# Placing pass of a graph kernel: two groups ahead on TensorE and ScalarE, one ahead on VectorE

## The reference

```python
for l in range(thetas.shape[0]):            # 3 layers
    xi, xj = x[src], x[dst]
    e = jax.nn.relu((xj - xi) @ thetas[l].T + xi @ phis[l].T)
    agg = jax.ops.segment_max(e, src, num_segments=N)
    agg = jnp.where(agg < -1e+30, 0.0, agg)
    mu, var = agg.mean(axis=0), agg.var(axis=0)
    x = jax.nn.relu((agg - mu) * jax.lax.rsqrt(var + BN_EPS) * gammas[l] + betas[l])
...
summ = jax.ops.segment_sum(msg, dst, num_segments=n)      # the later blocks sum over targets
```

## Time and profile before

| | us |
|---|---|
| median of three runs | 7011.9 (6974.34 to 7047.15) |
| the profiled execution, time | 7004.77 |
| its span, first to last instruction | 7003.0 |
| gathers of the second max-relative pass, first to last issue | 1298.8 to 1977.4 |

### The profile page before, as it was taken

One profiled execution on the slowest core, in us unless ns is written; L12 is line 12 of the kernel. 1 busy time (PEld: TensorE's weight loads), 2 busy tenths in 40 slices (PEclk: granted clock), 3 DMA queues, 4 the chain that ended last, 5 costly groups with the idle time before them and its releaser, 6 DMA issues. The chain is left out here.

```text
span 7003.0 us, 50568 instructions
## 1 busy us (share of the span) xinstructions
PE 2900.5 (41%) x12855; PEld 1680.4 (24%) x12907; DVE 3675.3 (52%) x8221; ACT 1725.5 (25%) x4386; POOL 3244.6 (46%) x3188
## 2 busy tenths in 40 slices
PE   4352001533354555699000597000300045677658
PEld 3211000311132222344000243000200024555435
DVE  8995444465555656444554433333543354565553
ACT  2270000122224555211232221323300022232222
POOL 0004776456536665100777301767277644555540
PEclk9696555755577777799555798555655567888879
DMA  0004554344434444233556433545255436878730
GB/s 8 1 1 148 184 187 161 101 153 168 157 109 140 160 161 151 94 153 139 178 195 208 167 134 136 197 168 193 92 181 193 167 131 203 270 260 276 248 98 19
DMA packets 379867, 1066.01 MB, mean 152 GB/s; under 512 B 74258, under 2 KB 162612, under 8 KB 333012
## 3 DMA queue, kind: packets, MB, share of 16 engines
q1 hardware_dynamic: 213586, 595.68, 22.6%
q0 software_dynamic: 164688, 466.32, 22.5%
q10 hardware_dynamic: 1330, 0.99, 0.0%
HBM read 541.40 MB, written 521.29 MB: 152 GB/s over the span
## 5 line engine op out<-in xcount | busy, mean ns | idle before, releaser
L790 POOL DMA_INDIRECT out_of<-table,index x936 | 966.5, 1033 | 706.6 <-DVE index L813 415.0
L790 POOL DMA_INDIRECT rows<-table,index x728 | 739.7, 1016 | 404.3 <-issue 217.4
L790 POOL DMA_INDIRECT rows<-typed_table,index x520 | 517.8, 996 | 587.2 <-DVE index L813 387.5
L3082 POOL DMA_INDIRECT qv<-qv_table,index x416 | 429.6, 1033 | 392.6 <-DVE index L3259 264.3
L790 POOL DMA_INDIRECT y<-typed_table,index x312 | 325.2, 1042 | 571.0 <-DVE index L813 462.7
L1460 PE MATMUL bank<-x,marks 128*128 128x416 f16 x1664 | 392.4, 400 | 315.2 <-ACT marks L1473 237.1
L825 DVE SCALAR_TENSOR_TENSOR y<-y,by_source_anew,out_of 128x256 f32<-128x256 f32 x897 | 436.4, 486 | 101.1 <-DMA out_of<-table,index 61.3
L1473 ACT ACTIVATE marks<-hot_block,x 128x128 f16<-128x128 f16 x1248 | 369.9, 386 | 346.0 <-DVE marks L1520 335.5
L2126 PE MATMUL bank<-weights,turned_y 128*128 128x512 f32 x800 | 357.5, 596 | 6.2 <-ACT turned_y L2186 5.5
L1933 PE MATMUL bank<-weights,out_of 128*128 128x512 f32 x800 | 349.7, 595 | 12.9 <-DVE weights L1978 12.9
L807 ACT ACTIVATE rows<-rows,by_target_weight 128x256 f32<-128x256 f32 x520 | 214.9, 494 | 518.8 <-DMA rows<-typed_table,index 270.0
(11 more groups left out here) (586 smaller groups left out, 7152.0 us busy)
## 6 DMA issues: line engine op xcount, KB each, us to landing
states<-y SPq DMA_DIRECT2D x156, 1024.0 KB
typed_table<-staged SPq DMA_DIRECT2D x400, 256.0 KB, 2.0
states<-state SPq DMA_DIRECT2D x78, 1024.0 KB
states<-out_of SPq DMA_DIRECT2D x78, 1024.0 KB
wide_states<-y SPq DMA_DIRECT2D x52, 1088.0 KB
near<-k_rows SPq DMA_DIRECT2D x416, 128.0 KB
out_of<-table,index POOLq DMA_INDIRECT x936
rows<-table,index POOLq DMA_INDIRECT x728
```

The costliest lines, as they stand in the source:

```text
L790: pool.indirect_dma_start(out=rows[h][:, u * D:(u + 1) * D], out_offset=None, in_=table, in_offset=bass.IndirectOffsetOnAxis(ap=index[h][: ...
L3082: pool.indirect_dma_start(out=qv[b][:, u * PAIR:(u + 1) * PAIR], out_offset=None, in_=qv_table, in_offset=bass.IndirectOffsetOnAxis(ap=ind ...
```

## The change

Each engine's order in PlaceTargets is shifted by whole groups.

- PE, in iteration g: codes and tally of group g+2, rank of g+1, compare of g+2, look_up of g.
- ACT, in iteration g: high half of g, then `hot_b` and `hot_r` of g+2.
- DVE, in the step of g: choose(g-1), mask(g+2), `part`(g), `run`(g), `same`(g+1), low(g).
- `hot_a` and `hot_r` get a third buffer.

The number of instructions and their shapes stay. Before the first group DVE now masks two groups and compares one.

The diff, cut to its core (the order of each engine):

```diff
             self.settle.tensor(pe)
-            over_groups(body)
+            for g in range(-2, GROUPS):
+                if g + 2 < GROUPS:
+                    meet(g + 2, g % 2)
+                    tally(g + 2, g % 2)
+                if 0 <= g + 1 < GROUPS:
+                    rank(g + 1, (g + 1) % 2)
+                if g + 2 < GROUPS:
+                    compare(g + 2, g % 2)
+                if g >= 0:
+                    pe.wait_ge(self.hot_row, 2 * g + 2)
+                    look_up(g, g % 2)
...
+            for g in range(-2, GROUPS):
+                if g >= 0:
+                    high(g, g % 2)
+                if g + 2 < GROUPS:
+                    mark(g + 2, g % 2)
...
     def mask(self, dve, g, h):
         nc, env, sort = self.sort.nc, self.sort.env, self.sort
-        if later(g):
+        if g >= 2:
             dve.wait_ge(self.crossed, 2 * g - 2)
+            dve.wait_ge(self.alike, 2 * g - 2)
...
-        self.mask(dve, 0, 0)
+        for g in range(2):
+            self.mask(dve, g, g)
+        self.match(dve, 0, 0)
         for g in range(RING + self.lead):
             self.group(dve, g, g % 2)
...
         if g > 0:
             self.choose(dve, g - 1, 1 - h)
-        if g < GROUPS - 1:
-            self.mask(dve, g + 1, 1 - h)
+        if g + 2 < GROUPS:
+            self.mask(dve, g + 2, h)
         dve.wait_ge(self.tallied, g + 1)
...
-        for s in range(2):
-            dve.wait_ge(self.alike, 2 * g + s + 1)
...
+        if g + 1 < GROUPS:
+            self.match(dve, g + 1, 1 - h)
         dve.wait_ge(self.cut_high, g + 1)
```

More of the change, by code:

```diff
@@ L1269, in ring @@
             return [buffer(stack, nc, name, cols, dt) for _ in range(count)]
-        self.mine, self.same, self.hot_b, self.hot_r = ring("mine", GROUP * P), ring("same", GROUP * P), ring("hot_b", GROUP * P), ring("hot_r", GROUP * P)
-        self.hot_a, self.run = ring("hot_a", GROUP * TILES), ring("run", TILES, FP32)
+        self.mine, self.same, self.hot_b, self.hot_r = ring("mine", GROUP * P), ring("same", GROUP * P), ring("hot_b", GROUP * P), ring("hot_r", GROUP * P, count=3)
+        self.hot_a, self.run = ring("hot_a", GROUP * TILES, count=3), ring("run", TILES, FP32)
         self.part, self.high_low, self.found = ring("part", GROUP * TILES, FP32), ring("high_low", 2 * GROUP * TILES), ring("found", 2 * GROUP * TILES, FP32)
@@ L1285, in _, with meet @@
         def _(pe):
-            def compare(g, h):
+            def meet(g, h):
                 now = sort.z[:, g * P:(g + 1) * P]
-                pe.wait_ge(self.masked, g + 1)
-                for s in range(2):
[L1290 to L1293, removed]
                 for s in range(2):
@@ L1353, in body @@
                     act.wait_ge(self.crossed, 2 * g + s + 1)
-                    if s == 0 and later(g):
-                        act.wait_ge(self.looked_up, g - 1)
-                    nc.scalar.activation(self.hot_r[h][:, s * half:(s + 1) * half], self.code_bank[s][:, 0:half], ACT.Relu,
+                    if s == 0 and g >= 3:
+                        act.wait_ge(self.looked_up, g - 2)
+                    nc.scalar.activation(self.hot_r[g % 3][:, s * half:(s + 1) * half], self.code_bank[s][:, 0:half], ACT.Relu,
@@ L1372, in mask, with match @@
-        hot_tiles(nc, env, self.hot_a[h][:], sort.col_a, g).then_inc(self.hot_tile, 1)
+        if g >= 3:
+            dve.wait_ge(self.picked, g - 2)
+        hot_tiles(nc, env, self.hot_a[g % 3][:], sort.col_a, g).then_inc(self.hot_tile, 1)
+    def match(self, dve, g, h):
+        nc, env = self.sort.nc, self.sort.env
+        half = GROUP * P // 2
+        for s in range(2):
+            dve.wait_ge(self.alike, 2 * g + s + 1)
+            if s == 0 and g >= 2:
+                dve.wait_ge(self.ranked, g - 1)
+            nc.vector.scalar_tensor_tensor(
+                out=bulk(self.same[h][:, s * half:(s + 1) * half], GROUP // 2), in0=bulk(self.alike_bank[s][:, 0:half], GROUP // 2),
+                scalar=float(NODE_BITS), in1=env.before[:].unsqueeze(1).broadcast_to([P, GROUP // 2, P]),
+                op0=ALU.is_equal, op1=ALU.mult).then_inc(self.compared, 1)
@@ L1407, in group @@
                                 op=ALU.add).then_inc(self.running, 1)
-        for s in range(2):
-            dve.wait_ge(self.alike, 2 * g + s + 1)
-            if s == 0 and later(g):
-                dve.wait_ge(self.ranked, g - 1)
-            nc.vector.scalar_tensor_tensor(
-                out=bulk(self.same[h][:, s * half:(s + 1) * half], GROUP // 2), in0=bulk(self.alike_bank[s][:, 0:half], GROUP // 2),
-                scalar=float(NODE_BITS), in1=env.before[:].unsqueeze(1).broadcast_to([P, GROUP // 2, P]),
-                op0=ALU.is_equal, op1=ALU.mult).then_inc(self.compared, 1)
+        if g + 1 < GROUPS:
+            self.match(dve, g + 1, 1 - h)
         dve.wait_ge(self.cut_high, g + 1)
```

34 lines of the change are left out of this document (16 added, 18 removed).

## The result

The changed kernel takes 7054.2 us (median of 20 runs, 7025.0 to 7091.4) against 7011.1 us for the kernel before on the same chip: 1.0068 times as long, 95% interval 1.0048 to 1.0087. That is 43 us slower, above the whole predicted range, which ended at 7025. The profiled execution has a span of 7070.2 us.

What follows compares the result with a forecast made beforehand. DVE with its waits for PE was taken to set the second max-relative pass's pace. From 7005 us, 56 gained in the loop and 6 lost before it gave 6955, or 6962 from the median; forecast 6960, range 6900 to 7025.

Steps and rivals of the forecast that it cites:

- part 3: Look-up in the second pass's loop: its 5.2 us chain fits 6.0 us; the wait before `found` is 70 to 100 us.
- Part 1: Tally asked for two groups ahead: DVE's 144.5 us of waits before `part` are gained, all but nothing left.
- Part 2: Comparison one group ahead and masks two ahead: `same` had no idle time before it, so nothing gained or lost.
- Part 4: Gathers come next in the loop: 530 to 550 us, middle 540, a gain of 56; ends 492 and 596.
- Part 5: Five groups before the loop, without a fold as cover: loss of 6 us, between a gain of 10 and a loss of 15.
- (a): Rival: the wait moves from `part` to `found`, DVE's 226 us of waits stay, loop 596 us, total 7015; chance 0.24.
- (b): Rival: gathers bound the loop at the pace of a pass without companion, 492 us, total 6910; chance 0.22.
- (c): Rival: look-up late in every group because of ACT's order, held codes, tally and look-up adding up; 7090 us, chance 0.08.

Runs made afterwards that it cites:

- e5: Changed kernel with seven of eight gathers of the second max-relative pass left out from its fifth group on; 6685.5 us, one run.
- v1: Changed kernel with TensorE's look-up of g right behind rank of g+1, ahead of compare, crossed and tally of g+2; 1.0059 of the kernel before.
- v4: Changed kernel with `hot_b` of g+2 ahead of the high half of g on ScalarE, `hot_r` still behind it; 1.0069 of the kernel before.
- e8: Changed kernel with POOL allowed three groups of gathers ahead of the folds in the second pass instead of four; 1.0063 of the kernel before.
- e10: Changed kernel with POOL stopped after every second group (16 gathers) of the second pass until the gathers have landed; 6832.8 us, 0.9873 of the kernel before.
- e18: The changed kernel as it is, run again on another chip; 6285.7 us, 1.0007 of the kernel before.
- e16: Changed kernel with POOL stopped after every fourth group (32 gathers) of the second pass; 1.0048 of the kernel before.
- v3: Changed kernel with look-up ahead of compare, crossed and tally, choose(g-1) ending VectorE's group, four buffers of `hot_a` and `hot_r`; 1.0023 of the kernel before.

## Why the prediction was wrong

**The step that failed is part 3, the look-up**, which took "70 to 100 us" for the wait before `found`, and bounded it by "all of the 144.5 us could come back here". It measured 261.3, above even the 70.0 + 144.5 = 214.5 of that bound. That the chain fits into its cover of 6.0 us was right, and e5 shows it: without most of the gathers `found` waits 0.6 us in all. (The 5.2 us of the chain are rather 5.4: rank, compare and look-up of the earlier trace rows are 0.37 + 1.03 + 0.51 = 1.9 us, not 1.7.) What was wrong was the nature of a hold. I took it from the earlier trace rows as a delay of 5 to 6 us that adds to one operation and can be hidden by asking two groups ahead. It is more like a closed door: reports of TensorE pile up, and most of the long ones come only when POOL has run out of gathers. In the table of reports above tally, rank, compare, look-up and codes were issued within 2.0 us; the first was learned of 16.1 us after its issue and the other six within 0.23 us of each other, 1.5 us later. Asking earlier does not help against that, as v1 to v4 show.

Why the sum of the waits grew, from 214.5 to 261.3 us, is argued and not shown. DVE can run ahead only over reports that are already in, and while it does, it writes indices and so gives POOL more gathers; that this keeps the door shut for longer fits the 14 waits over 10 us now against 4 before, and e8 did not confirm it. What the traces do show is the price of a stop. POOL stood still for over 0.9 us 22 times in the loop now, for 7.8 us on average, and 21 times for 5.7 us before: 172 against 119 us, which is the loop's loss of 47 us and a little more. Part of it is the place of the wait. When `found` has ended a long wait, the rest of DVE's step and the next fold lie between it and the next index, and POOL issues again 8.8 us later. In the kernel before this was 6.8 us after six of its waits before `part`, and 9.7 after three before `found`.

**Part 1** was right: `part` waits 0.0 us. **Part 2** was right: `same` 0.0, masks 0. **Part 4** fell with part 3: a loop of 540 us was forecast, 644 came. That e10 took 534 us is luck: its length is made of gathers and added stops, which the forecast did not have. On the chip of e18 the loop is 468, below the end of 492 that was given. **Part 5** had 6 us and the rows of the stretch show 15, of which 4 lie in the groups themselves.

**The rivals.** (a), "the wait only changes its place", is the mechanism that came nearest: what was paid at `part` is paid at `found`. Its price of 7015 kept the sum of the waits at 226 us. They became 261.3 + 12 = 273: the waits are now fewer and longer (26 of 9.2 us instead of 31 of 6.4 at both lines). (c) put its turning point at 4.8 us a group before `found`; 261.3 / 47 = 5.6 passed it, and the result lies between its 7040 and its 7090. But its reason, the place of the look-up behind the tally and ScalarE's order, was undone by v1 and by v4 without any gain. That 7054 lies about as near to its price of 7090 (36 us) as to that of (a) (39 us) is luck: its cause is not there. (b), gathers as the bound, is what happened on the chip of e18, and gave the change nothing there either: the kernel before took 6279 us and the changed one 6286.

The prediction set aside a rule of the Trainium skill, "SBUF — State Buffer", section "Who interferes with whom", by which PE never waits on anyone and DMA never contends with a compute engine. That section is about the ports of SBUF and says nothing of when a finished matmul is reported; that by it no completion would be held was the prediction's own step. The runs show reports that are held 5 to 16 us with gathers in flight, and no wait for them with most of the gathers left out (after against e5); they show no matmul that was slowed at a port. So they neither bear the rule out nor speak against it.

**What stays open.** What closes the door: reports held are shown, by 0.034 us between two of 512 columns; through what they pass together with the gathers is not. Why three chips hold reports (6911 to 6993 us for the kernel before) and one does not (6279). What ends the holds that end with gathers still being issued: most of the kernel before's, up to 10.7 us, and one of 15.4 us in the changed kernel; that the old order's shorter look-ahead keeps POOL closer to running dry, so that doors open oftener, fits e10 and e16, but e8 did not confirm it. And whether the kernel before waits as little as e18 on that chip, since only its total was measured there.

The fastest version on chips that hold is the changed kernel, or v3, with a stop after every second group of the second pass, 0.987 of before; the old order with the same stops, 0.989, is as good within what was measured. On the chip that does not hold, stops in two passes cost 2.2%, of which the 74 us of the second pass are 1.2.

## What to carry to other kernels

A wait that only shows while another engine's transfers run is first to be taken with those transfers left out: one such run here (`found` 261.3 to 0.6 us) told more than four that changed the order. Looking further ahead is meant for a delay that belongs to an operation. Against one that lasts as long as a condition does it gained nothing here, and the waits even grew, from 214.5 to 261.3 us. And where a remedy rests on such a condition, it is to be timed on more than one chip: stops in one pass gave 1.3% on one, and stops in two passes cost 2.2% on another.

## What was not expected of the hardware

Reports of TensorE came up to 16 us after the matmuls they belong to, several in a row within 0.2 us, in order, with the first of them 0.7 us and the others 2.1 to 2.4 us after the last gather had landed (1895.07 to 1895.745, 1897.195 and 1897.425); the longest wait for one was 24.1 us, in v1. Stores of SP at 49.3 MB in 376 us held none (e5). VectorE was not held meanwhile: the folds went on at 0.49 us each. One chip of four showed nothing of it, and ran the kernel before 9 to 10% faster than the others; in its pass without a companion a gather took 1.33 us, against 589 / 416 = 1.42 in the profile of the changed kernel above. Inside the loop the spacing of gathers without a stop between them was nearly the same on all: 1.27 us in the changed kernel, 1.30 in e10 and in e18.
